# A graph layer's last scaling on GpSimd: one broadcast multiply, or one instruction for each row with the scale as a column

## The reference, cut to what matters

```
x = layernorm(x + attention(x, edges))            # (x - mean) / sqrt(var + eps), over 256 features
x = layernorm(x + concat(x, messages) @ W + b)    # again
```

## Time and profile before

| | us |
|---|---|
| median of 3 runs | 1115.83 (1112.52 to 1116.24) |
| the profiled execution | 1115.02 |
| its span, first to last instruction | 1113.3 |
| PE busy | 1046.2 (94%) |
| DVE busy | 949.6 (85%) |
| POOL busy | 810.9 (73%) |
| ACT busy | 779.0 (70%) |

### The profile page before, as it was taken

One profiled execution on the slowest core, in us unless ns is written; L12 is line 12 of the kernel. 1 busy time (PEld: TensorE's weight loads), 2 busy tenths in 40 slices (PEclk: granted clock), 3 DMA queues, 4 the chain that ended last, 5 costly groups with the idle time before them and its releaser, 6 DMA issues.

```text
span 1113.3 us, 25449 instructions
## 1 busy us (share of the span) xinstructions
PE 1046.2 (94%) x7204; PEld 971.6 (87%) x7204; DVE 949.6 (85%) x2692; ACT 779.0 (70%) x2403; POOL 810.9 (73%) x656
## 2 busy tenths in 40 slices
PE   5888999999999999999978899989999999999993
PEld 4778999999999999999857788879989898889982
DVE  5878888888889988888999799768888888888882
ACT  3876777777777777777859698856666666666663
POOL 5588888888888788885888798735666666666663
PEclk9999999999999999999989899989999999999997
DMA  4876766666666666665545467765666666666640
GB/s 154 304 248 217 231 231 231 231 230 228 230 231 232 217 228 229 232 230 194 209 151 209 151 229 263 251 192 164 172 173 187 191 180 192 185 182 191 189 139 34
DMA packets 121388, 227.26 MB, mean 204 GB/s; under 512 B 33587, under 2 KB 61486, under 8 KB 121184
## 3 DMA queue, kind: packets, MB, share of 16 engines
q1 hardware_dynamic: 104000, 189.54, 51.8%
q0 software_dynamic: 17248, 36.08, 10.9%
HBM read 137.84 MB, written 93.59 MB: 208 GB/s over the span
## 4 chain that ended last, share of the span: by engine, by line
PE 55%; DVE 23%; issue 9%; ACT 6%; SPq 2%; DMA 1%; DVEq 1%; POOL 0%; ACTq 0%; POOLq 0%
PE ps L852 7%; PE ps L831 5%; DVE num L1619 5%; PE ps L891 5%; PE ps L892 4%; PE ps L893 4%; PE ps L845 4%; PE ps L846 4%; PE ps L847 4%; DVE zeT L1630 3%; DVE est L1656 3%; DVE agg L1643 3%; ACT t L1192 2%; DVE msg L1639 2%; PE ps L913 2%
## 5 line engine op out<-in xcount | busy, mean ns | idle before, releaser
L682 POOL TENSOR_TENSOR zin<-xin,bff_row 128x1024 f32<-128x1024 f32 x98 | 232.9, 2377 | 36.4 <-DVE stat L1409 17.4
L1437 DVE SCALAR_TENSOR_TENSOR yn<-ps,r,bc 128x256 f32<-128x256 f32 x391 | 169.1, 473 | 60.4 <-PE ps L847 38.3
L852 PE MATMUL ps<-w_mix,zT 128*128 128x256 f32 x780 | 188.5, 392 | 10.2 <-ACT zT L1093 5.5
L852 PEld LDWEIGHTS ps<-w_mix,zT 128*128 128x128 f32 x780 | 146.9, 196 | 34.3 <-ACT zT L1093 10.8
L1108 ACT ACTIVATE junk<-yn 128x256 f32<-128x256 f32 x391 | 157.9, 415 | 10.9 <-DVE yn L1437 10.8
L743 POOL TENSOR_TENSOR ev<-abc,v 128x512 f32<-128x512 f32 x49 | 62.1, 1268 | 115.9 <-DVE zeT L1630 113.6
L1409 DVE BATCH_NORM_STATS2 stat<-zin 128x6 f32<-128x256 f32 x391 | 135.3, 407 | 1.9 <-issue 1.5
L724 POOL DMA_INDIRECT ty<-in_node_type_dram,src_i x98 | 103.3, 1054 | 25.7 <-issue 23.5
L755 POOL DMA_INDIRECT out_dram<-oe,idx x98 | 100.6, 1027 | 25.4 <-issue 20.4
L845 PE MATMUL ps<-mix_hi,z_hi 128*128 128x256 f32 x392 | 114.6, 292 | 2.8 <-DVE z_lo L1474 2.8
L736 POOL DMA_INDIRECT xs<-in_x_dram,idx x98 | 93.4, 953 | 29.6 <-issue 29.3
(11 more groups left out here) (212 smaller groups left out, 3339.5 us busy)
## 6 DMA issues: line engine op xcount, KB each, us to landing
xin<-in_x_dram SPq DMA_DIRECT2D x97, 512.0 KB, 4.1
out_dram<-on SPq DMA_DIRECT2D x97, 512.0 KB
xd_o<-xdT SPq DMA_DIRECT2D x49, 256.0 KB, 2.0
v_o<-vT SPq DMA_DIRECT2D x49, 256.0 KB
v<-v_o SPq DMA_DIRECT2D x49, 256.0 KB
xd<-xd_o SPq DMA_DIRECT2D x49, 256.0 KB, 4.2
abc<-a_o SPq DMA_DIRECT2D x196, 64.0 KB
sbc<-same_o SPq DMA_DIRECT2D x49, 128.0 KB, 3.8
```

The costliest lines, as they stand in the source:

```text
L682: pool.tensor_tensor(z, xx, bb, ALU.add).then_inc(n_z, 1)
L852: last = mm(ps[0:np_, half(g, j), (j % 2) * D:(j % 2 + 1) * D], zT[:, g % 2, k, j * P:j * P + np_], w_mix[:, k, :], start=k == 0, stop=k = ...
L1437: last = dve.scalar_tensor_tensor(out=yn[0:np_, q, j * D:(j + 1) * D], in0=ps[0:np_, half(g, j), (j % 2) * D:(j % 2 + 1) * D], scalar=r1[0 ...
```

## The change

Only `final` of GpSimd differs. Before, one `tensor_tensor` multiplies all of POOL's rows of a group by `r2`, broadcast along each row of 256. After, a loop issues one `tensor_scalar` for each row, whose scalar operand is a column of `r2` (one value for each partition). The wait ahead and the semaphore behind (now on the last row's instruction) are the same. So 49 instructions become 113: 33 pairs, 15 threes, and a pair on 112 partitions.

```diff
         def final(g):
             q = g % SLOTS
             np_, nj = size(g)
-            n = nj - split(g)
             pool.wait_ge(n_r2, g + 1)
             after(pool, n_out[q], 16 * (g // SLOTS))
-            rows = [a[0:np_, q, split(g) * D:nj * D].rearrange("p (j d) -> p j d", j=n) for a in (on, yn)]
-            scale = r2[0:np_, q, split(g):nj].rearrange("p (j a) -> p j a", a=1).to_broadcast([np_, n, D])
-            pool.tensor_tensor(rows[0], rows[1], scale, ALU.mult).then_inc(n_od, 1)
+            for j in range(split(g), nj):
+                last = pool.tensor_scalar(on[0:np_, q, j * D:(j + 1) * D], yn[0:np_, q, j * D:(j + 1) * D],
+                                          r2[0:np_, q, j:j + 1], None, ALU.mult)
+            last.then_inc(n_od, 1)
```

## The result

The change makes the kernel slower: 1130.17 us (median of 4 runs, 1130.05 to 1130.98) against 1115.84, a ratio of 1.0130 with a 95% interval of 1.0107 to 1.0154. The prediction said 1113.4, between 1109 and 1120.

A forecast was written before the change was run, and what follows sets the result against it. PE was taken to set the pace from 650 to 735 us; at the start and in the softmax, DVE waits for POOL. Terms 0.5 + 0.5 + 0.25 + 0.5 + 0.3 = 2.05 us gave 1113.4 us, range 1109 to 1120.

The forecast's parts named there:

- The price of a row: GpSimd's `final`: a row of 256 takes 0.412 us, priced from `neg_a`, so two rows get 0.25 us shorter.
- The upper bound: GpSimd's `final`: at 2.13 ns an element a row takes 0.75 us, two rows 1.46, 0.42 longer than before.
- The places where `final` counts: Start 0.5, softmax finals from 534.43 us 0.5, before `z_add` at 559.60 0.25, at 605.84 and 610.36 0.5, end 0.3 us.
- the slower rival: Start, softmax, 17 turns and end: POOL becomes pace-setter from about 0.6 us a row, 5.7 us lost, 1121; chance 0.16.
- against it: Softmax, three places: a later `z_add` lets DVE go first, gaining some 2 us each time, which would reverse the loss.
- The finals of three rows: Fifteen finals in the stretch that PE sets: they gain nothing, since `z_add` of 2.36 and `final` of 1.46 us leave POOL idle.
- The forecast's own sum: Start, softmax and end: shorter finals save 0.5 + 0.5 + 0.25 + 0.5 + 0.3 = 2.05 us.
- The clock at the start: Start: a shorter idle time keeps TensorE's clock up, 1.7 us more, 3.75 in all, 1111.7; chance 0.20.
- the forecast's 0.5 to 1.0 us: Start, four finals from 58.00 to 82.21 us: two count surely and two perhaps, 0.5, at most 1.0 us gained.

The follow-up runs named there:

- the kernel with two operations: The changed kernel with a second operation, plus constant 0.0, in each of GpSimd's row instructions: 0.9980 of the time before the change.
- the kernel with five forms: Kernel for durations only: GpSimd's row instruction takes five forms (constant or column, one or two operations) in five stretches of groups; one execution of 1111.56 us.

## Why the prediction was wrong

**The price of a row, the step that failed.** "A row then takes 0.201 + 0.211 = 0.412 us. ... I take 0.25, since `neg_a` is the same operation; the column instead of a constant is what is not shown." `neg_a` is not the same operation: it multiplies and adds, the change only multiplies. With the second operation and constants the row does take 0.404 us; with one operation it takes 0.85, with the column 0.92. I looked for the doubt in the operand, where 0.07 us was to be found, and not in the operation, where 0.45 was. The upper bound failed with it: I took the rate of the two-tensor add, 2.13 ns an element, as the worst, and the lone multiply runs at 2.6.

The page that I set aside, "GPSIMD Engine Reference" of the Trainium skill, "Elementwise — side-by-side cycle accounting", pointed the right way: a `final` that gets longer. My estimate from its figure, 1.14 us for two rows, is far from the 1.84 measured. Its 1.5 ns an element, the best of a software loop there, lies between the two rates measured: two operations with constants run at (937 - 404) / 640 = 0.83 ns, below that best, and one operation at 2.6.

**The places where `final` counts.** These were right, with the sign turned. The start paid 3.5 to 3.9 us (four finals, each longer by 0.8, is 3.2); the stretch from 534 to 567 did not pay, since VectorE went first, as the slower rival's "against it" had it (that `z_add`'s delay "would turn the loss round"); behind it the statistics wait for `z_add`, 2.9 us in all from 600 to 680 and 16.2 from 680 on.

**The finals of three rows.** "The other finals gain nothing, above all the fifteen of three rows" holds for a gain. For a loss it misled: my slower rival counted the start, the middle and the end, but not these. And the reason given there, that `z_add` and `final` "leave POOL idle in each turn", was a misreading. In the kernel before POOL works without a pause from 677.12 to 692.40, in turns of 3.75 us; its idle time lies behind that, 2.86 us before each of the finals at 720.83 and 725.15:

```profile
683.43 1.46 POOL L721 TENSOR_TENSOR on<-yn,r 128x768 f32<-128x768 f32 x1
684.86 2.36 POOL L682 TENSOR_TENSOR zin<-xin,bff_row 128x1024 f32<-128x1024 f32 x1
687.19 1.46 POOL L721 TENSOR_TENSOR on<-yn,r 128x768 f32<-128x768 f32 x1
...
720.83 1.47 POOL L721 TENSOR_TENSOR on<-yn,r 128x768 f32<-128x768 f32 x1 [2.86 <-DVE r L1447]
725.15 1.47 POOL L721 TENSOR_TENSOR on<-yn,r 128x768 f32<-128x768 f32 x1 [2.86 <-DVE r L1447]
```

These two are 4.32 us apart, with PE busy for all 14 us from 716 to 730: that is TensorE's turn, and one of 2.36 + 2.7 us is longer. In the changed kernel the three-row groups behind the copy of the types add 5.7 us to POOL's lag; alone they cost 0.4%, 4.5 us.

**The slower rival** named the mechanism that came: GpSimd as the pace-setter, deciding from 0.6 us a row. At 0.75 it gave 1121; at 0.92, with the three-row turns that it lacked, it is 1130. Its bound was too low: rows of 0.62 us (the broadcast multiply row by row) made the kernel 0.3% faster, rows of 0.85 made it 0.5% slower.

**The forecast's own sum** can be judged by the kernel with two operations. There a final of two rows saves 0.12 us (2 x 0.47 - 0.03 = 0.91 instead of 1.04), so half of the forecast's 2.05 us, 0.1%; measured is 0.2%, interval 0.06 to 0.34%. The size agrees, the places do not show it: in that kernel's trace DVE waits 4.82 us for POOL at the start, not less than 4.41, and `next_c` still takes 3.11.

**The clock at the start**, the faster rival, can be judged by the kernel with five forms, whose rows in the start take 0.404 us, the forecast's price. Its timeline, and the window behind the idle time:

```profile
80.67 0.48 DVE L1465 TENSOR_SCALAR_CACHE_REDUCE on<-yn,r 128x256 f32<-128x256 f32 x1 [2.70 <-POOL on L722]
...
83.95 0.36 PE L901 MATMUL ps<-w_hi,xd_hi 128*128 128x256 f32 x1 [1.43 <-issue]
```

```profile
83.95:87.95 4.00, 4.00 (x34) 4.00 (x35) 3.90 (x13) 1.71 (x4) 3.05 (x4) 1.00 0.68 228
```

DVE waits 2.70 us where the forecast had 3.9 or less, the clock is up, and the softmax begins at 525.4 instead of 531.1: with the row's price right, the start alone would have given more than the forecast's 0.5 to 1.0 us. This is one execution, of 1111.56 us; how much of it is the clock that an unchanged start can have too was not separated.

## What to carry to other kernels

Before a row of one operation is priced by another of the same name, see that both have the same number of operations; here a `tensor_scalar` on GpSimd that only multiplies or adds f32 rows costs twice one with two operations, so try a second operation that does nothing. An engine that is off the critical path in the chain of waits can still be one queue position away from it: look for the turns where it is never idle, and work out from which duration on it sets the pace, for all shapes, also those that gain nothing. And where two engines exclude each other, a delay of a tenth of a microsecond decides which goes first; such a gain is real only when the whole time shows it. A mark from one profiled execution needs the same mark from other kernels that are alike up to there, before a difference is read from it.

## What the runs showed of the hardware that I had not expected

GpSimd's `tensor_scalar` on 128 x 256 f32: one operation 0.85 us (constant) and 0.92 (column), 2.6 ns an element from 256 to 512; two operations 0.40 and 0.47. The multiply of a tensor with a broadcast column takes 0.62, so it beats the one-operation form.

A VectorE instruction on two SBUF tensors and GpSimd's add exclude each other in both directions: `next_c` takes 1.05 us when it comes 0.03 us first, and `z_add` then 3.25 instead of 2.36; 3.20 and 2.36 in the other order. The page "SBUF — State Buffer" of the Trainium skill, section "Who interferes with whom", says this: the two engines share one pair of ports under an exclusive lock, an instruction of VectorE with two SBUF inputs contends for it, and the order of issue decides who blocks. The traces agree.
